# Two-layer Perceiver block on one core: larger blocks, a longer lag and a shared addition in the two cross-attentions

## The reference

```python
q, k, v = heads(Q @ W_Q + b_Q), heads(K @ W_K + b_K), heads(V @ W_V + b_V)   # 16 heads of 32
scores = einsum('bhqd,bhkd->bhqk', q, k) / sqrt(32)                          # 512 x 8192 per head
attn = softmax(scores, axis=-1)
out = einsum('bhqk,bhkd->bhqd', attn, v)
x = x + merge_heads(out) @ W_O + b_O
```

## Time and profile before

| | us |
|---|---|
| median of 3 runs | 3646.66 |
| lowest, highest | 3643.27, 3648.98 |
| the profiled execution | 3645.09 |
| its span, first to last instruction | 3643.3 |
| TensorE busy in the span | 3527.5 (97%) |
| VectorE busy | 2497.3 (69%) |
| ScalarE busy | 1967.2 (54%) |
| Pool busy | 1773.3 (49%) |

### The profile page before, as it was taken

One profiled execution on the slowest core, in us unless ns is written; L12 is line 12 of the kernel. 1 busy time (PEld: TensorE's weight loads), 2 busy tenths in 40 slices (PEclk: granted clock), 3 DMA queues, 4 the chain that ended last, 5 costly groups with the idle time before them and its releaser, 6 DMA issues. The chain is left out here.

```text
span 3643.3 us, 47301 instructions
## 1 busy us (share of the span) xinstructions
PE 3527.5 (97%) x17916; PEld 2334.9 (64%) x17916; DVE 2497.3 (69%) x3465; ACT 1967.2 (54%) x3024; POOL 1773.3 (49%) x744
## 2 busy tenths in 40 slices
PE   8999999999999999988999999999999897999999
PEld 6788787755555555446876555555554476788887
DVE  3222344478777777457996777777775565899998
ACT  2122322366666666634972666666666322777786
POOL 2222222399999999700000999999998320100001
PEclk9999999999999999998998999999999998999999
DMA  7777776633333333046977433333330101999998
GB/s 272 253 243 235 234 239 208 190 79 91 93 90 77 88 93 77 15 174 223 359 302 238 122 92 84 80 93 93 80 91 24 53 1 53 361 377 374 374 375 302
DMA packets 249729, 628.50 MB, mean 173 GB/s; under 512 B 43633, under 2 KB 137873, under 8 KB 194977
## 3 DMA queue, kind: packets, MB, share of 16 engines
q1 hardware_dynamic: 210720, 552.08, 46.8%
q10 hardware_dynamic: 36864, 67.13, 5.0%
q0 software_dynamic: 1920, 6.29, 0.5%
HBM read 488.46 MB, written 136.87 MB: 172 GB/s over the span
## 5 line engine op out<-in xcount | busy, mean ns | idle before, releaser
L780 DVE TENSOR_REDUCE maxima<-psum 128x1 f32<-128x512 f32 x2048 | 1263.4, 680 | 359.3 <-PE psum L775 359.1
L920 ACT ACTIVATE pt<-psum 128x512 f32<-128x512 f32 x2048 | 1047.7, 612 | 590.6 <-PE psum L797 587.9
L932 POOL TENSOR_TENSOR exp_sums<-pt 128x1024 f32<-128x1024 f32 x342 | 819.3, 2396 | 259.2 <-ACT pt L920 136.9
L775 PE MATMUL psum<-ks,first_q 96*128 96x512 f32 x2048 | 852.4, 416 | 0.8
L797 PE MATMUL psum<-qs,ks 97*128 97x512 f32 x2048 | 817.7, 406 | 12.2 <-ACT pt L920 9.1
L935 POOL TENSOR_TENSOR exp_sums<-exp_sums,pt 128x1024 f32<-128x1024 f32 x310 | 735.7, 2373 | 44.5
L810 PE MATMUL psum<-pt,vs 128*32 128x512 f32 x4096 | 673.9, 598 | 2.1 <-POOL exp_sums L932 1.9
L814 PE MATMUL psum<-exp_sums,constants 128*32 128x512 f32 x1408 | 669.8, 598 | 0.0
L775 PEld LDWEIGHTS psum<-ks,first_q 96*128 96x128 f32 x2048 | 390.0, 190 | 354.2 <-DVE maxima L780 236.2
L1631 DVE TENSOR_TENSOR moe_cut<-moe_raw,moe_cut 128x2048 fp32r<-128x2048 f32 x244 | 556.8, 2289 | 55.9 <-ACT moe_cut L1627 49.5
L1627 ACT CAST moe_cut<-moe_raw 128x2048 fp32r<-128x2048 f32 x244 | 469.0, 1923 | 56.2 <-PE psum L97 47.3
(11 more groups left out here) (334 smaller groups left out, 4526.5 us busy)
## 6 DMA issues: line engine op xcount, KB each, us to landing
moe_raw<-in_moe_w SPq DMA_DIRECT2D x244, 1024.0 KB, 7.9
ks<-k_parts SPq DMA_DIRECT2D x384, 256.0 KB, 4.6
k_parts<-kparts ACTq DMA_DIRECT2D x256, 256.0 KB, 4.4
cx<-in_ctx SPq DMA_DIRECT2D x32, 1024.0 KB, 6.1
vs<-v_heads SPq DMA_DIRECT2D x32, 1024.0 KB, 5.3
v_heads<-vrow SPq DMA_DIRECT2D x25, 1024.0 KB, 5.1
late_context<-cparts SPq DMA_DIRECT2D x28, 512.0 KB, 11.6
late_parts<-late_context SPq DMA_DIRECT2D x28, 512.0 KB, 4.7
```

What stands on the lines that cost most here:

```text
L775: pe.matmul(self.c.bank[self.FIRST_BANK + k % self.FIRST_ROOM], self.first_q[s][:, t * P:(t + 1) * P], self.ks[s][part][0:3 * DH, at:at + ...
L780: dve.tensor_reduce(self.maxima[:, h % 2, i % TT, i // TT:i // TT + 1], self.c.bank[self.FIRST_BANK + k % self.FIRST_ROOM], X, ALU.max).th ...
L920: act.activation(self.pt[:, self.slot(h, b) + i, :], self.c.bank[self.SECOND_BANK + n % self.SECOND_ROOM], ACT.Exp).then_inc(*self.exp.up())
L932: engine.tensor_tensor(to, self.pt[:, slot:slot + R, :], self.pt[:, slot + R:slot + 2 * R, :], ALU.add).then_inc(*signal.up())
```

## The change

Blocks become six of nine tiles and one of ten (the tenth goes in a round of its own: one value product and one ones-product). Pool makes three tiles of nine by two additions of 128 x 1536. In blocks 1, 3 and 5 of all heads but the last, the second of these additions is split: Pool adds two of the three tiles, and VectorE the third (128 x 512, after the maximum three tiles past the block's end, when Pool's first addition is done). A block is weighed 12 tiles after its last tile, where that falls in the order of tiles; the ring has 24 slots. The order on all engines is now written by tile: one maximum product and one score product per tile.

The head's end changes: four transposes of the partial result instead of the fold (after tile 16 of the next head), then on VectorE the reciprocal, a multiplication of all three partial sums (4 x 96) and a reduction that adds the three (after tile 17). The bias bv is added by ScalarE when it copies the turned heads. The constant `fold` is gone.

```diff
-    ROUNDS, LAG = 2, 2
-    BLOCKS = [list(range(t, min(t + 3 * 2, KT))) for t in range(0, KT, 3 * 2)]
+    ROUNDS, LAG = 3, 12
+    BLOCKS = [list(range(t, t + 3 * 3)) for t in range(0, KT - 10, 3 * 3)] + [list(range(KT - 10, KT))]
+    STRIDE, RING = 66, 24
+    TAKE, TURN = LAG, LAG + 4
+    SHARED, SHARE_AT = (1, 3, 5), 3
-    RING = (LAG + 1) * BLOCK
-    EARLY_PRODUCTS = [(), (), (), (), (0,), (1,), (2,), (3,), (4,), (5, 6), (7, 8)]
+    COPY_AT = (10, 15, 20)
+    EARLY_AT = {3: (0, ()), 8: (1, ()), 13: (2, ()), 26: (None, (0,)), 32: (None, (1,)), 38: (None, (2,)), 43: (None, (3,)), 48: (None, (4,)), 53: (None, (5, 6)), 58: (None, (7, 8))}
...
+    def slot(self, h, t):
+        return (h * self.STRIDE + t) % self.RING
+    def due(self, h, t, late):
+        n = h * KT + t - late
+        return [(n // KT, b) for b, tiles in enumerate(self.BLOCKS) if n >= 0 and n % KT == tiles[-1]]
+    def first_to(self, h, t):
+        n = self.UNITS + h * KT + t + 1 + self.AHEAD - (6 * (KT - 1 - t) // (KT - 7) if h == 0 else 0)
+        return min(len(self.slots), max(self.EARLY, n))
...
         def weigh(h, b):
...
             if b == 0 and h:
-                pe.wait_ge(*self.finished.at(h))
+                pe.wait_ge(*self.divided.at(h))
             pe.wait_ge(*self.exp.at(h * KT + tiles[-1] + 1))
-            if self.adds(b):
-                pe.wait_ge(*self.sums_to(h, b))
+            if not self.on_vector(h, b):
+                pe.wait_ge(*self.sum_pool.at(self.sums_by_pool(h, b)))
+            if self.on_vector(h, b) or self.shared(h, b):
+                pe.wait_ge(*self.sum_dve.at(self.sums_by_dve(h, b)))
+            rounds = [tiles[i:i + 3] for i in range(0, len(tiles), 3)]
...
         def finish_head(h):
             pe.wait_ge(*self.taken.at(h + 1))
             for t in range(TT):
-                last = pe.matmul(bank[self.OUT_BANK][:, t * (DH + 1):(t + 1) * (DH + 1)], self.partial[:, t * P:(t + 1) * P], c.fold[:], start=True, stop=True)
+                last = pe.transpose(bank[self.OUT_BANK][:, t * P:(t + 1) * P], self.partial[:, t * P:(t + 1) * P], c.ident[:])
...
+            for t in range(KT):
+                for k in range(begun, self.first_to(h, t)):
                     self.first_on_pe(pe, k)
-                if b >= self.LAG:
-                    weigh(h, b - self.LAG)
-                elif h:
-                    weigh(h - 1, NB - self.LAG + b)
+                begun = self.first_to(h, t)
+                second_on_pe(h, t)
+                if h + 1 == HEADS and t in self.EARLY_AT:
+                    output_early(*self.EARLY_AT[t])
+                if t == self.TURN and h:
+                    finish_head(h - 1)
+                for block in self.due(h, t, self.LAG):
+                    weigh(*block)
...
         for h in range(HEADS):
             head(h)
-        for b in range(NB - self.LAG, NB):
-            weigh(HEADS - 1, b)
+        for t in range(KT, KT + self.LAG):
+            for block in self.due(HEADS - 1, t, self.LAG):
+                weigh(*block)
...
-            act.copy(self.at[:, k, :], self.c.bank[b]).then_inc(*self.at_copied.up())
+            if k == 0:
+                act.wait_ge(*self.wo_in.at(3))
+            act.activation(self.at[:, k, :], self.c.bank[b], ACT.Identity, bias=self.bv[:, k:k + 1]).then_inc(*self.at_copied.up())
...
+    def add_up(self, engine, h, b, n, signal, parts=range(3)):
+        g, tiles, lo, hi = h * len(self.BLOCKS) + b, self.BLOCKS[b], parts[0], parts[-1] + 1
+        later = self.slot(h, tiles[3 * n + 3])
+        to = self.sums[:, g % 2, lo:hi]
+        engine.wait_ge(*self.exp.at(h * KT + tiles[3 * n + 3] + hi))
         if n == 0:
             if g > 1:
                 engine.wait_ge(*self.weighed.at(g - 1))
+            first = self.slot(h, tiles[0])
+            engine.tensor_tensor(to, self.pt[:, first + lo:first + hi, :], self.pt[:, later + lo:later + hi, :], ALU.add).then_inc(*signal.up())
         else:
-            engine.wait_ge(*signal.at(signal.total - signal.base))
+            engine.tensor_tensor(to, to, self.pt[:, later + lo:later + hi, :], ALU.add).then_inc(*signal.up())
...
+            dve.tensor_tensor(self.scaled[:].rearrange("p t g d -> p t (g d)"), turned[:, :, 0:3 * DH], self.total[:, :, None].to_broadcast([P, TT, 3 * DH]), ALU.mult).then_inc(*self.divided.up())
+            dve.wait_ge(*self.divided.at(h + 1))
+            dve.tensor_reduce(self.rows[:, :, h * DH:(h + 1) * DH], self.scaled[:].rearrange("p t g d -> p t d g"), X, ALU.add).then_inc(*self.finished.up())
...
+            for t in range(KT):
+                for k in range(begun, self.first_to(h, t)):
                     self.first_on_dve(dve, k)
+                begun = self.first_to(h, t)
+                if t == self.TURN + 1 and h:
+                    finish_head(h - 1)
+                for i, b in self.due(h, t, self.SHARE_AT):
+                    if self.shared(i, b):
+                        dve.wait_ge(*self.sum_pool.at(self.sums_by_pool(i, b) - 1))
+                        self.add_up(dve, i, b, 1, self.sum_dve, range(2, 3))
...
     def on_pool(self, pool):
         for h in range(HEADS):
             for b in range(len(self.BLOCKS)):
                 if not self.on_vector(h, b):
-                    for n in range(self.adds(b)):
-                        self.add_up(pool, h, b, n, self.sum_pool)
+                    self.add_up(pool, h, b, 0, self.sum_pool)
+                    pool.wait_ge(*self.sum_pool.at(self.sums_by_pool(h, b) - 1))
+                    self.add_up(pool, h, b, 1, self.sum_pool, range(2) if self.shared(h, b) else range(3))
```

More of the change, by code:

```diff
@@ L536, in __init__, with shared, blocks_to, sums_by_pool @@
         self.c, self.A, self.S, self.x, self.l, self.late = c, A, S, x, l, late
-        self.slots, self.upto = self.first_slots()
+        self.slots = [(h, i) for h in range(HEADS) for i in range(self.UNITS)]
         self.begun, self.keys_stored = 0, []
-    def adds(self, b):
-        return -(-len(self.BLOCKS[b]) // self.ROUNDS) - 1
     def on_vector(self, h, b):
         return h + 1 == HEADS and b % 2 == 1
[L548 to L555, removed]
+    def shared(self, h, b):
+        return h + 1 < HEADS and b in self.SHARED
+    def blocks_to(self, h, b):
+        return [(i, j) for i in range(h + 1) for j in range(len(self.BLOCKS)) if (i, j) <= (h, b)]
+    def sums_by_pool(self, h, b):
+        return 2 * sum(not self.on_vector(*g) for g in self.blocks_to(h, b))
+    def sums_by_dve(self, h, b):
+        return sum(2 if self.on_vector(*g) else self.shared(*g) for g in self.blocks_to(h, b))
+    def slot(self, h, t):
[6 more added lines that the diff above has]
+        return min(len(self.slots), max(self.EARLY, n))
     def hold(self, st):
@@ L752, in loads @@
                     self.load_k(sp, h + 2, part)
[L754 to L762, removed]
     def first_on_pe(self, pe, k):
@@ L799, in weigh @@
         def weigh(h, b):
-            tiles, slot, sums = self.BLOCKS[b], self.slot(h, b), (h * NB + b) % 2
+            tiles, sums = self.BLOCKS[b], (h * NB + b) % 2
             if b == 0:
@@ L803, in weigh @@
             if b == 0 and h:
-                pe.wait_ge(*self.finished.at(h))
+                pe.wait_ge(*self.divided.at(h))
             pe.wait_ge(*self.exp.at(h * KT + tiles[-1] + 1))
-            if self.adds(b):
-                pe.wait_ge(*self.sums_to(h, b))
[L808 to L814, removed]
+            if not self.on_vector(h, b):
[3 more added lines that the diff above has]
+            rounds = [tiles[i:i + 3] for i in range(0, len(tiles), 3)]
+            for r, three in enumerate(rounds):
+                for g, t in enumerate(three):
+                    pe.matmul(bank[self.OUT_BANK][g * DH:(g + 1) * DH, :], vs[h % 2][:, t, :], pt[:, self.slot(h, t), :], start=b == 0 and r == 0, stop=t + 3 >= KT)
+                item = self.sums[:, sums, r, :] if r < self.ROUNDS else pt[:, self.slot(h, three[0]), :]
+                last = pe.matmul(bank[self.OUT_BANK][3 * DH:4 * DH, :], c.ones[:, 0:DH], item, start=b == 0 and r == 0, stop=b == NB - 1 and r == len(rounds) - 1)
             last.then_inc(*self.weighed.up())
@@ L970, in on_dve @@
+                for i, b in self.due(h, t, 0):
+                    if self.on_vector(i, b):
+                        self.add_up(dve, i, b, 0, self.sum_dve)
+                        dve.wait_ge(*self.sum_dve.at(self.sums_by_dve(i, b) - 1))
+                        self.add_up(dve, i, b, 1, self.sum_dve)
         finish_head(HEADS - 1)
```

95 lines of the change are left out of this document (31 added, 64 removed).

## The result

The change makes the kernel slower. The median of four runs is 3665.90 us against 3644.97 of four runs of the kernel before beside them: ratio 1.0055, 95% interval 1.0043 to 1.0068. I had 3620 and a range of 3598 to 3660. The profiled executions differ by 3667.14 - 3645.09 = +22.05 us, where the forecast was -25.2: 47.2 us are to be found.

A forecast was written before the change was run, and what follows sets the result against it. TensorE was taken to set the pace, with Pool at 93% close behind. Terms of -38.4, -13.2, +2.8, +18.2 and +5.4 sum to -25.2, taking 3645.1 to 3620 us; range 3598 to 3660.

The forecast's parts named there:

- What bounds the kernel: In the 14 heads TensorE, busy 745.8 of 746.7 us, sets the pace; Pool at 93% is close behind.
- Term 1: Eleven blocks per head become seven, saving four weighings of 0.32 us: -1.28 us per head, -38.4 in all; no stall.
- Term 2: End of a head: transposes replace folding, -13.2 us; weighing waits for VectorE's multiplication, +2.8 us.
- Term 3, block 1: VectorE comes at 7.1, after Pool's second addition starts; the late reductions cost TensorE 0.65 us x 28 heads, +18.2.
- Term 3, blocks 3 and 5: VectorE is first at the port by 0.11 us; Pool waits 0.6 us that it has; TensorE pays nothing.
- rival A: Pool wins the port in blocks 3 and 5 too: +66 us, 3688; chance 0.13 whole, 0.12 in one block (3654).
- Term 4: At the very end TensorE waits some 3.7 us for Pool's block 6 sums: +2.7 per layer, +5.4.
- At nothing: Bias on ScalarE's last-head copies, L950's removal, narrower bv load and smaller constants in the first head: counted as no cost.
- Pool's rate and who blocks: Pool's 1536 addition takes 3.50 us by the rows, 3.33 by the reference; issue order decides who blocks at the port.

The follow-up runs named there:

- experiment 1: The changed kernel with VectorE's share taken out in all blocks, Pool adding all three tiles: 3618.65 us.
- experiment 6: The kernel before with only the new end of a head, blocks of six and Pool's additions as before: 3635.33 us.
- experiment 8: The changed kernel without shares, ones casts at tiles 21, 30, 39, 48, last head's even blocks on VectorE, L795 after block 5's turn: median 3594.19 us, ratio 0.9865.
- experiment 5: The changed kernel with VectorE adding the last head's even blocks, block 6 among them, instead of the odd ones: 3652.32 us.
- experiment 11: The changed kernel run once more, unchanged, for the spread of head 0 and its clock: 3665.29 us.
- Experiment 7: The changed kernel with VectorE's shares in blocks 2, 3 and 4 instead of 1, 3 and 5: 3617.20 us.

## Why the prediction was wrong, step by step

- **What bounds the kernel:** right. TensorE stays busy for over 99.5% of the 14 heads; what is lost is lost in it, as products that start later.
- **Term 1, fewer weighings, -1.28 us per head: right.** The comparison of experiments 1 and 6 gives 1.28. That it is the same to the last digit is luck: experiment 1 holds L795's cost, and the new end of a head gives 0.30 in long runs and 0.12 in experiment 6, and these two cancel. Undisturbed runs of nine take 7.10 against my 7.11. What I wrote about the runs (no stall, nothing spare) holds too. But I didn't ask what else stands on VectorE in such a run. L795 costs 0.18 us per head there (7.31 to 7.13 in experiment 8), 26 x 0.18 = 4.7 us that no term had.
- **Term 2, the end of a head, -0.34 net: nearly right.** A run with it takes 7.71, one without 7.10, so 0.61 against 0.91 before (5.77 - 4.86): -0.30. Alone, in blocks of six, it gives 0.12.
- **Term 3, block 1, +0.65: right in mechanism and size.** VectorE came at 7.24 after the run's start (forecast 7.1) and Pool let go at 8.36 (8.4); the price was 0.52. I had left out L959, which stands ahead of it in heads 1 to 4, where it was 0.85.
- **Term 3, blocks 3 and 5, "VectorE is first by 0.11 us; TensorE pays nothing": the step that failed, for block 5.** In block 3 it is right, with half the margin. VectorE starts 0.04 after Pool's end, near the 0.03 of the earlier trace rows, but Pool's own next addition comes after 0.08 and not the 0.14 of the earlier trace rows. In block 5 I counted nine reductions and not the L795 among them. It makes VectorE 0.26 us later (a run of nine reductions takes 5.73 with it and 5.47 without), more than the margin. VectorE came 6.18 after the run's start and Pool's second addition began at 5.99. The price is 8.04 - 7.13 = 0.91 in 26 of the 28 heads, 23.7 us, half of the whole miss. That is my rival A for one of two blocks, priced 1.1, but for a cause that stood in neither the forecast nor the rival: a margin of 0.1 us wants every instruction of the engine in that stretch listed.
- **Term 4, the tail, +2.7 per layer: right in its wait (3.44 against 3.7), short in its total.** The last head grew by 3.3. The wait grew by 2.5 (0.97 to 3.44); the clock behind it added 1.8, which no term had; and the last head without its wait became 0.9 faster (49.9 - 0.97 = 48.9 to the 48.0 of experiment 5), where I had 0.44 for the end of a head.
- **"At nothing": wrong for head 0.** I didn't name L744, two of whose casts now fall into runs (some 1.2 us in each layer; the cast at tile 12 waited before too), nor the clock at the start of the attention, which holds 10.1 - 5.1 = 5.0 us in layer 0. Head 0 also has shares, which no term had (1.2 and 0.9, from experiment 1). That is 9.5 of its 11.7; about 2 us stay open. Most of the clock's part is chance: in experiment 11 the same kernel lost 6.4 us by it and not 10.1.
- **The sum:** of 30.0 us missed in the 2 x 14 heads, block 5 holds 23.7, L795 4.7, term 2 1.1, one fall of the clock 1.7, and block 1 -1.0 (20 x 0.52 + 8 x 0.85 = 17.2 against 18.2), together 30.2. 3.4 us outside the attentions are not explained and no larger than what those stretches vary by.
- **Pool's rate and who blocks:** the GPSIMD Engine Reference of the Trainium skill (Performance versus the Vector engine) gave an estimate of 3.33 us for Pool's 1536; the trace has 3.49, and my value from the earlier trace rows was 3.50. By 3.33 I had called blocks 3 and 5 a toss; block 3 was none, and block 5 was decided by L795. SBUF — State Buffer of the Trainium skill (Who interferes with whom) says that issue order decides who blocks. The shares agree: 0.69 us when VectorE is first, 1.66 and 2.74 when Pool is.

## What to carry to other kernels

When two engines compete for the same memory behind one event, list everything that stands on each of them in that stretch; a small operation that comes once per head decided some 24 us here. A share handed to another engine is free only where that engine is already waiting when the event comes, so place it by the block, not by the count: the same three additions cost 1.4 us per head in blocks 1, 3 and 5 and nothing in 2, 3 and 4. And before a difference at the start of a stage is put down to an edit, run the unchanged kernel again: the clock alone moved head 0 by 3.3 us.

## What the runs showed of the hardware

- Behind the same completion of Pool, VectorE's addition starts 0.04 us later and Pool's own next 0.08 us later. When VectorE is first, Pool's addition of 1024 grows from 2.36 to 2.90 us; when Pool is first, VectorE's of 512 lasts until Pool's ends and 0.55 us longer, against 0.69 alone.
- Pool's addition of 128x1536 takes 3.49 us and VectorE's of the same shape 1.76 us.
- After TensorE's wait of 3.44 us at the end, the granted clock fell to half in most traces but not in all (15 of 18 attentions). Experiment 7 shows both, with the same wait: layer 0 (first row) and layer 1.

```profile
1542.00:1547.00 5.00, 4.89 (x28) 1.58 (x28) 0.00 (x0) 0.00 (x0) 0.00 (x0) 0.66 0.02 3
2821.00:2825.00 4.00, 3.59 (x28) 1.04 (x28) 0.00 (x0) 0.38 (x1) 0.00 (x0) 1.00 0.00 0
```

The last head took 53.2 us with the fall and 51.4 without it. What decides between the two these runs don't show. Such a fall also came behind waits of 1.37 and 0.41 us, and in the last of the 14 intervals behind one of 0.22 only, where TensorE had been busy 4.70 of 5 us (2802 to 2807 us of the kernel after); each is some 3.4 us at half speed, 1.7 us lost.
